# Eight scores and their exponentials issued beside the last context pieces, in the banks of the maxima

## The reference

```python
q = (x1 @ wq.T)   # 2 x 1024 tokens, 16 heads of 32
k = (x2 @ wk.T)   # 2 x 2048 context rows
v = (x2 @ wv.T)
dots = einsum('bhnd,bhmd->bhnm', q, k) * SCALE
attn = softmax(dots, axis=-1)
out = einsum('bhnm,bhmd->bhnd', attn, v)
```

## Time and profile before

| | us |
|---|---|
| median of 3 executions | 1896.85 (1895.04 to 1898.93) |
| the profiled execution, whole | 1896.42 |
| its span, first to last instruction | 1894.6 |
| TensorE busy in the span | 1872.4 (99%) |
| VectorE busy | 1252.0 (66%) |
| ScalarE busy | 893.1 (47%) |
| GpSimd busy | 827.5 (44%) |

### The profile page before, as it was taken

The page is one execution under the profiler, slowest core; times in us unless marked ns, Lnnn a source line. Parts: engine busy times, 40 slices in busy tenths (PEclk is TensorE's granted clock), DMA queues, the critical chain, the costliest instruction groups (busy, mean ns, idle before and its releaser), DMA issues.

```text
span 1894.6 us, 26849 instructions
## 1 busy us (share of the span) xinstructions
PE 1872.4 (99%) x10104; PEld 1285.2 (68%) x10104; DVE 1252.0 (66%) x2354; ACT 893.1 (47%) x1601; POOL 827.5 (44%) x745
## 2 busy tenths in 40 slices
PE   9999999999999999999999999999989999999998
PEld 8886787788555555555445545544459998899986
DVE  6675574277777788888778778778654444444447
ACT  4312323221666666666456456546734433344333
POOL 4002201000587888888667657666012233222232
PEclk9999999999999999999999999999999999999999
DMA  8003525684767585757644525442234454444544
GB/s 284 23 1 117 186 98 177 203 242 145 153 134 168 114 198 127 167 108 165 137 117 102 135 53 143 112 98 76 85 114 145 137 134 116 116 108 129 149 106 156
DMA packets 124498, 250.13 MB, mean 132 GB/s; under 512 B 11312, under 2 KB 29504, under 8 KB 119680
## 3 DMA queue, kind: packets, MB, share of 16 engines
q1 hardware_dynamic: 109696, 187.56, 33.2%
q0 software_dynamic: 14672, 60.85, 15.7%
HBM read 148.46 MB, written 62.42 MB: 111 GB/s over the span
## 4 chain that ended last, share of the span: by engine, by line
PE 88%; DVE 10%; issue 1%; POOL 0%; DMA 0%; ACT 0%; SPq 0%; DVEq 0%; POOLq 0%; ACTq 0%
PE banks L1204 39%; PE banks L1512 12%; PE banks L1399 11%; PE banks L1369 11%; PE banks L1388 9%; DVE max L1727 8%; PE banks L1420 4%; PE banks L1210 2%; PE banks L1300 1%; DVE den_c L1746 0%; PE banks L1377 0%; POOL xg L2273 0%; PE banks L1486 0%; DMA xg<-x_rows,tok 0%; DMA raw<-in_wk_t 0%
## 5 line engine op out<-in xcount | busy, mean ns | idle before, releaser
L1727 DVE TENSOR_REDUCE max<-banks 128x1 f32<-128x512 f32 x1024 | 628.2, 682 | 129.8 <-PE banks L1369 129.0
L2235 POOL TENSOR_TENSOR probs<-probs,probs 128x512 f32<-128x512 f32 x464 | 583.2, 1293 | 232.4 <-PE banks L1399 232.4
L2113 ACT ACTIVATE probs<-banks 128x512 f32<-128x512 f32 x1024 | 521.5, 607 | 259.2 <-PE banks L1388 258.4
L1369 PE MATMUL banks<-k_stack,q_stack 98*128 98x512 f32 x1024 | 429.2, 426 | 0.0
L1388 PE MATMUL banks<-q_stack,k_stack 98*128 98x512 f32 x1024 | 377.3, 399 | 2.6 <-ACT probs L2113 2.6
L1369 PEld LDWEIGHTS banks<-k_stack,q_stack 98*128 98x128 f32 x1024 | 192.1, 188 | 191.8 <-DVE max L1727 108.2
L1399 PE MATMUL banks<-probs,v_grp 128*32 128x512 f32 x2048 | 250.5, 601 | 0.0
L1388 PEld LDWEIGHTS banks<-q_stack,k_stack 98*128 98x128 f32 x1024 | 192.2, 189 | 59.7 <-ACT probs L2113 15.9
L2282 POOL DMA_INDIRECT y_rows<-eo,tok x35 | 71.7, 2050 | 169.7 <-DVE eo L1940 121.1
L1927 DVE TENSOR_TENSOR hid_lo<-hid,hid_hi 128x640 fp32r<-128x640 f32 x64 | 52.7, 824 | 126.4 <-ACT hid_hi L2182 126.4
L1399 PEld LDWEIGHTS banks<-probs,v_grp 128*32 128x32 f32 x2048 | 60.0, 109 | 108.4 <-issue 102.2
(11 more groups left out here) (268 smaller groups left out, 2817.1 us busy)
## 6 DMA issues: line engine op xcount, KB each, us to landing
k_stack<-k_parts SPq DMA_DIRECT2D x144, 256.0 KB, 5.2
probs<-probs POOLq DMA_DIRECT2D x36, 1024.0 KB, 9.9
w_raw<-in_L_ffn_w SPq DMA_DIRECT2D x16, 2048.0 KB, 8.2
q_stack<-q_parts SPq DMA_DIRECT2D x48, 256.0 KB
v_grp<-v_rows SPq DMA_DIRECT2D x48, 256.0 KB, 3.5
raw<-in_ctx_t SPq DMA_DIRECT2D x8, 1024.0 KB, 6.2
k_parts<-out_hi SPq DMA_DIRECT2D x32, 256.0 KB, 2.6
k_parts<-out_lo SPq DMA_DIRECT2D x32, 256.0 KB, 3.0
```

The source lines that it names most:

```text
L1369: nc.tensor.matmul(out, queries_of(t)[:, j, tile_of(k)], keys_of(t)[0:STK + SHIFT, j, mc * HALF:(mc + 1) * HALF], start=True, stop=True) \
L1727: V.reduce_max(max4[:, tiles_of(t), :, :][:, k, j, mc:mc + 1], bank(bank_of["max", t, mc, k, j]), AX.X) \
L2113: S.activation(probs_of(t, s)[:, j, :], bank(bank_of["score", t, s, j]), ACT.Exp, scale=SCALE) \
L2235: G.tensor_tensor(a[:, j, :], a[:, j, :], b[:, j, :], ALU.add).then_inc(pair_added.sem, 1)
```

## The change

The 8 scores of turn 0, steps 0 and 1, are taken from behind the context and put at the end of the generator `first_maxima`, behind the 32 maxima ahead, with the gate before them. They use the ring of banks 4 to 7 (`side_bank`), as the maxima there do. The number of units that `together` spreads over main units 12 to 61 rises from 97 to 105. What stood behind the scores, `second_stack()` and its gate, now stands directly behind the context's last unit.

```diff
@@ first_maxima
                     for c in range(VQ):
                         load_v(0, c)
                 yield
+            plan.append(("gate_loop", "loop"))
+            for s in range(2):
+                for j in range(HG):
+                    do("score", 0, s, j, ring=side_bank)
+                    yield
@@
         attention_end = [x.now() for x in first_part]
-        together(context(1), first_maxima(), MAX_UNITS + MAXIMA_AHEAD + 1, 3 * NG, CONTEXT_UNITS - 2)
         gates["loop"] = attention_end
-        plan.append(("gate_loop", "loop"))
+        together(context(1), first_maxima(), MAX_UNITS + MAXIMA_AHEAD + 2 * HG + 1, 3 * NG, CONTEXT_UNITS - 2)
@@
-        for s in range(2):
-            for j in range(HG):
-                do("score", 0, s, j, ring=next_score_bank)
         second_stack()
         max_bank = next_s_bank
```

## The result

The changed kernel takes 1899.47 us in the median of 22 executions (1896.57 to 1901.58), the kernel before 1896.80 (22 executions): a ratio of 1.0015, 95% interval 1.0009 to 1.0021, so 1.7 to 4.0 us slower. The profiled execution has a span of 1898.5 us against 1894.6. The change loses time where it was meant to win some.

The account below looks back on a forecast made before the run. TensorE was taken to bound the kernel; 0.56 us net from the waits behind the context plus 1.05 us of lower clock made 1.6 us more, 1896.42 to 1898.0 us, range 1894.0 to 1901.0.

Parts of the forecast that it names:

- rival 1: At the loop's start, the forecast itself: gate stall and lower clock together cost +0.8 to +2.3 us; chance 0.58.
- rival 4: Half clock goes beyond one spell, slowing first `num` and next block: +2.6 on top, +4.2, 1900.6 us; chance 0.13.
- What bounds, and that nothing absorbs the delay: Whole kernel: TensorE, busy 99% of the span, bounds it; later blocks neither absorb nor add to the 1.6 us.
- Moved scores wait for nothing: Among context matmuls, 8 scores in four banks run without waiting; their stall of 1.89 us goes.
- The context: Waits on the shift and loop gate, and earlier key chunk 3, cost nothing: 0, key chunk bounds 0 and 1 us.
- The copy out of bank 3: Behind the context, the first loop max waits for ScalarE's copy of the last value piece, until T + 0.84.
- The gate: VectorE's late passing holds the fourth max 2.71 us, until T + 4.96; with the copy's wait, net 0.56 us more.
- some 0.5 us: At the loop's gate, moved into the context: the cost of a list of satisfied waits if there were no cover.
- The clock: Around the stall before the first `num`, the clock falls again for some 3.3 us, costing 1.05 us.
- The 1.40 us "to be won": Behind the old scores, 484.17 to 487.45 us, half clock made 8 matmuls take 3.28 us for 1.88: 1.40 lost.
- Rival 2: The stall is there, but the clock doesn't fall or falls where TensorE stands anyway: +0.56, 1897.0 us; chance 0.17.
- Rival 3: No stall, VectorE passes the gate before it is needed: the full 3.29 us are won, 1893.1 us; chance 0.12.

Follow-up runs that it names:

- the later gate alone: Changed kernel, with VectorE, ScalarE and GpSimd meeting the second key stack's gate, and VectorE its memsets, only behind the loop's first block: 1895.68 us, 0.9996.
- the gate moved in the kernel before: Kernel before, with only the gate (not SyncE's wait) and VectorE's memsets put behind the loop's first block: 1896.54 us, 1.0001.
- bank 4 first in the changed kernel: Changed kernel, gate in place, with the loop's maxima using banks 4, 5, 3 in turn instead of 3, 4, 5: 1899.79 us, 1.0018.
- 16 fillers: Changed kernel with 16 added matmuls of 128 columns, results unused, ahead of the loop's fourth max: 1899.34 us, 1.0011.
- ScalarE's gate later: Changed kernel with ScalarE alone meeting the gate behind the loop's first block, VectorE standing at it as in the changed kernel: 1899.89 us, 1.0017.
- the fillers: Changed kernel with 8 added matmuls of 128 columns, results unused, ahead of the loop's fourth max: 1896.83 us, 1.0003.
- the later gate with bank 4: Changed kernel, gate behind the loop's first block for all but SyncE, loop's maxima beginning with bank 4: 1893.40 us (0.9984), repeated 1894.09 (0.9983).

## Why the prediction was right

The forecast was 1898.0 us, 1.6 above the profiled execution before; measured are 2.7 above the median. Direction, place and mechanism held: the gate holds the fourth max, and the clock falls behind it. Two terms were off in opposite directions, the gate's 0.58 us too high and the clock's 1.3 too low, so the sum is nearer than its larger part; that is luck. The measured size lies between rival 1 (+0.8 to +2.3) and rival 4 (+4.2).

- **What bounds, and that nothing absorbs the delay:** right. From the first max of the second block to the last `num` TensorE takes 897.11 us before (1388.41 − 491.30) and 897.00 after (1391.61 − 494.61). Medians follow the seam only loosely: taken against the kernel before, the two differ by 0.3 to 0.8 us in six kernels, and by 1.5 to 2.2 in five (the later gate alone, the gate moved in the kernel before, bank 4 first in the changed kernel, 16 fillers, ScalarE's gate later).
- **Moved scores wait for nothing:** right, 1.89 us of stall gone from the scores.
- **The context:** no wait of TensorE there. Key chunk 3 was issued from 421.87 to 424.06 and landed within 6.2 us of each issue, before its first max at 430.82. The price of 0 was right.
- **The copy out of bank 3:** 0.69 us idle, max at T + 0.85 (484.08 − 483.23), expected 0.84. But while the gate stands there it has no price of its own, as bank 4 first showed; with the gate moved it has one, 0.96 us of seam.
- **The gate:** expected the fourth max at T + 4.96 and a stall of 2.71 us; measured T + 4.34, with a stall of 1.84 us by the profile (2.0 from the end of the last matmul's slot). 0.45 of the 0.62 us is VectorE's passing: its memset came at T + 3.42 instead of T + 3.87. Before, VectorE got through 0.56 us behind SyncE, now 0.13 us behind. The traces' records of VectorE's semaphore waits show why. Before, six more of them follow the one that ends with the store (483.55), 0.098 us apart, up to 484.18; after, only two follow it (486.37), up to 486.57. Five others, the loop's gate, now lie in the context, from 473.43 to 473.87. So the "some 0.5 us" that the prediction gave such a list without cover was part of the old timeline, and the change removed it. The other 0.17 us is the first max, which began 0.24 us behind the first memset and not 0.36. At full clock the first `num` was to come at T + 7.73; with the fillers, which hold the clock, it came at T + 7.15.
- **The clock:** the step that was mis-sized. I took 1.05 us and one spell as long as the old one. The profile has 6.8 us at half, and the price is 13.26 − 10.88 = 2.38 us. I had put the second spell into rival 4, with a chance of 0.13, and priced it at 2.6 us on top. By that rival's own sign, a clock still low when `num` begins, it is what happened in this execution (`num` at 492.14, the clock low until 493.4); but it ended within `num`, where I had let it run over all of it and the next block. (The bound "up to 1.7" for `num` was also a slip: 3.48 − 1.92 is 1.56.) Other executions of like kernels had one spell. The gate's term was 0.58 too high (7.73 − 7.15) and the clock's 1.3 too low, which makes the 0.8 between 1.6 and the measured 2.36.
- **The 1.40 us "to be won":** right for that execution, not shown for the kernel. The kernel before with its gate moved has the same stretch without the fall. Against that seam the stall alone, at full clock, costs 10.88 − 9.72 = 1.16 us; against the profiled kernel before it seems to cost nothing (10.88 against 10.90), because that execution paid for a fall of its own.
- **Rival 2** (no fall) is what the fillers made: 1.0003, 0.7 us more by the medians where +0.56 was computed. **Rival 3** (no stall) is what the later gate with bank 4 made: 3.17 us off the seam, against 3.29 computed.

The rule of *DMA: Bandwidth & Descriptors* in the Trainium skill, "Rules for kernel authors", on computing between a transfer and its wait, fits what was measured: 2.5 us lie between the store's issue (484.05) and the gate's opening (486.52), as before (481.23 and 483.71), and they show on TensorE only without work in between.

## What to carry to other kernels

Before work is moved ahead of a boundary, look at what it covered behind it: work that waits inefficiently may stand over another engine's gate, and then moving it wins only if the gate moves too. Put a gate on the engines that need it and behind the first work that doesn't; here that took the loss of 2.7 us away, and with one bank chosen otherwise as well it made a gain of about 2.8. Price a stall of TensorE with the clock behind it: here the lower clock cost more (2.4 us of seam) than the stall (1.2).

## What the runs showed of the hardware

- The same stretch of 8 matmuls in 3.6 to 3.8 us was followed by the lower clock in one execution (0.50 from about 484 us on the earlier trace rows) and not in another, of the kernel before with its gate moved (1.00). A single profile doesn't tell what a thin stretch costs.
- After a stall of 0.69 and 1.84 us with six matmuls between, the clock stayed at 1.2 GHz for 6.8 us, though TensorE was busy in all of the last 3 us of it; a stall ending at nearly the same place, in four kernels with bank order, share of scores or gate varied, was followed by 3.4 us.
- With sixteen matmuls of 128 columns (eight calls, 1.95 us) in the stall, the clock stayed at 2.4 GHz in the profiled execution; the mean over the kernel's ten executions is 0.9978, against 0.9959 over the changed kernel's 22.
- Waits that are already satisfied are not free on VectorE: its wait records follow each other at 0.098 us, so the six behind the store's took 0.6 us before, and the two after the change 0.2 us.
